# Two sets of expert rows, V's products in two halves, and a new order of small steps, in a fused attention and expert kernel

## The reference

```
h   = layernorm(x)
q   = elu(h Wq) + 1;  k = elu(ctx Wk) + 1;  v = ctx Wv       # 16 heads of 8 features
out_t = (sum over s <= t of (q_t . k_s) v_s) / cumsum(q)_t    # causal, per head, element by element in q
x   = x + out Wo
h2  = layernorm(x)
bids = sigmoid(h2 conf_w' + conf_b) * wealth                  # 8 experts
the two best experts of each token, weights softmax(two best bids)
x   = x + sum over the two of weight * down_e(silu(gate_e h2) * up_e h2)    # inner width 512
```

## Time and profile before

| | us |
|---|---|
| median of 3 runs | 433.47 |
| lowest, highest | 432.7, 433.85 |
| the profiled execution | 430.86 |
| its span, first to last instruction | 429.1 |

### The profile page before, as it was taken

How to read it: one execution, slowest core, us unless ns; L and a number is a source line. 1 busy time by engine, 2 the same in 40 slices (tenths; PEclk the granted TensorE clock), 3 DMA queues, 4 the chain that set the end, 5 groups by cost and what they waited for, 6 DMA issues and landing times.

```text
span 429.1 us, 12428 instructions
## 1 busy us (share of the span) xinstructions
PE 319.4 (74%) x4413; PEld 264.9 (62%) x4413; DVE 288.5 (67%) x769; ACT 217.4 (51%) x440; POOL 212.2 (49%) x342
## 2 busy tenths in 40 slices
PE   3658788785988868586821089999999999999600
PEld 2537475654757756475520079999989989877400
DVE  5476999869796897989518247667657657633345
ACT  2591938347354573933122046766766766644300
POOL 4200223737364375666675406666666667664500
PEclk9896989688755899988555579999999999999855
DMA  8103030411404013010011333233233233221088
GB/s 270 63 2 124 2 124 4 128 48 34 141 15 152 12 33 107 20 33 27 26 44 44 115 49 78 61 74 70 60 76 70 61 72 66 51 51 23 4 273 314
DMA packets 45129, 32.36 MB, mean 75 GB/s; under 512 B 32262, under 2 KB 38796, under 8 KB 45072
## 3 DMA queue, kind: packets, MB, share of 16 engines
q1 hardware_dynamic: 40752, 23.12, 19.6%
q0 software_dynamic: 4320, 8.47, 6.3%
HBM read 15.16 MB, written 12.21 MB: 64 GB/s over the span
## 4 chain that ended last, share of the span: by engine, by line
issue 29%; POOL 28%; DVE 17%; PE 10%; DMA 8%; ACT 3%; SPq 3%; POOLq 1%; DVEq 0%; ACTq 0%
POOL by_token L488 12%; POOL by_expert L421 10%; DMA by_expert<-token_rows,rows_to 4%; DVE Pm L712 3%; DVE Vexp L695 2%; PE scores L954 2%; PE bank L938 2%; DVE stats L647 2%; DMA w_hi<-by_token 2%; POOL y_scale L483 2%; PE bank L970 2%; POOL rstd L392 1%; POOL y_to L484 1%; SPq L347 1%; DVE oT L719 1%
## 5 line engine op out<-in xcount | busy, mean ns | idle before, releaser
L488 POOL DMA_INDIRECT by_token<-y_sb,y_to x71 | 83.3, 1173 | 26.4 <-issue 24.8
L894 DVE TENSOR_TENSOR Kexp<-hid,hid_hi 128x512 f16<-128x512 f32 x71 | 48.8, 688 | 47.9 <-ACT hid_hi L626 47.7
L421 POOL DMA_INDIRECT by_expert<-token_rows,rows_to x64 | 65.1, 1017 | 22.1 <-issue 22.1
L888 DVE SCALAR_TENSOR_TENSOR hid<-scores,silu 128x512 f32<-128x512 f32 x71 | 48.8, 688 | 24.9 <-PE scores L1074 24.9
L619 ACT ACTIVATE silu<-bank 128x512 f32<-128x512 f32 x71 | 42.3, 596 | 34.4 <-PE bank L1074 33.8
L1072 PE MATMUL bank<-xgT,w_hi 128*128 128x256 f16 (+1 forms) x160 | 42.4, 266 | 17.7 <-DMA xgT<-by_expert 16.5
L954 PEld LDWEIGHTS scores<-qT,Kexp 32*128 32x128 f32 x1024 | 39.6, 229 | 25.3 <-DVE Pm L712 22.7
L1089 PE MATMUL bank<-w_hi,hid_hi 128*128 x284 | 51.4, 220 | 2.5 <-DVE Kexp L894 2.5
L954 PE MATMUL scores<-qT,Kexp 32*128 32x128 f32 (+1 forms) x1024 | 44.5, 322 | 10.7 <-DVE Pm L712 10.7
L1091 PE MATMUL bank<-w_hi,Kexp 128*128 x284 | 51.0, 219 | 0.0
L1090 PE MATMUL bank<-w_lo,hid_hi 128*128 x284 | 50.9, 219 | 0.0
(11 more groups left out here) (148 smaller groups left out, 689.2 us busy)
## 6 DMA issues: line engine op xcount, KB each, us to landing
w_raw<-in_w_pack_dram SPq DMA_DIRECT2D x8, 768.0 KB, 4.9
x_all<-in_x_tok_dram SPq DMA_DIRECT2D x8, 256.0 KB, 5.2
cT<-in_ctx_t_dram SPq DMA_DIRECT2D x8, 256.0 KB, 5.4
w_hi<-by_token SPq DMA_DIRECT2D x4, 512.0 KB, 7.2
w_lo<-by_token SPq DMA_DIRECT2D x4, 512.0 KB, 7.6
out_dram<-x_all SPq DMA_DIRECT2D x8, 256.0 KB, 5.8
by_expert<-pad_row SPq DMA_DIRECT2D x9, 130.0 KB, 2.7
by_token<-y_sb,y_to POOLq DMA_INDIRECT x71, 2.7
```

Of the source, the lines that this page charges most:

```text
L421: pool.indirect_dma_start(by_expert, bass.IndirectOffsetOnAxis(ap=rows_to[:, s, b:b + 1], axis=0), token_rows[:, b, s, :], None).then_inc( ...
L488: pool.indirect_dma_start(by_token, bass.IndirectOffsetOnAxis(ap=y_to[:, kk, s:s + 1], axis=0), y_sb[:, kk, s, :], None, bounds_check=NT * ...
L888: dve.scalar_tensor_tensor(hid[:, slot, :], bank[2 + slot], 1.0 / WSCALE, silu[:, slot, :], ALU.mult, ALU.mult).then_inc(hid_done, 1)
L894: dve.tensor_tensor(hid_lo[:, k % 2, slot, :], hid[:, slot, :], hid_hi[:, k % 2, slot, :], ALU.subtract).then_inc(lo_done, 1)
```

## The change

The two buffers `token_rows` and `rows_to` become two each, used by even and odd units in turn, with a semaphore `dispatched` for each. ACT and DVE now wait in the tail of unit u for the dispatch of unit u-2, where they waited for that of unit u-1. ACT's `tail_norm` gets a wait for POOL's `tail_rows` of unit u-2, which reads the `x2hat` that is overwritten. `front_values` is called once for each half: the first half (bank 1) directly behind `values(u, 1)`, the second where the whole was. PE's `tail_x2` goes ahead of `values(u, 1)`. On ACT the first two `front_keys` go ahead of `front_copy_x`, `tail_norm` ahead of the exponentials of q, and `tail_x2` ahead of the last two `front_keys`. DVE's `front_v` waits for each half.

```diff
--- before.py
+++ after.py
@@ -119,12 +119,12 @@
         region = sb("region", [P, E])
         rank = sb("rank", [P, UB, E])
         place = sb("place", [P, TOP, UB, E])
-        rows_to = sb("rows_to", [P, TOP, UB], U32)
+        rows_to = [sb(f"rows_to{i}", [P, TOP, UB], U32) for i in range(2)]
         pair_id = sb("pair_id", [P, UB, TOP])
         unit_ids = sb("unit_ids", [P, UB, TOP])
         unit_start = sb("unit_start", [P, UB, TOP])
-        token_rows = sb("token_rows", [P, UB, TOP, ROW])
-        row_halves = token_rows[:].rearrange("p b s r -> p (b s r)").bitcast(F16).rearrange("p (b s r) -> p b s r", b=UB, s=TOP)
+        token_rows = [sb(f"token_rows{i}", [P, UB, TOP, ROW]) for i in range(2)]
+        row_halves = [rows[:].rearrange("p b s r -> p (b s r)").bitcast(F16).rearrange("p (b s r) -> p b s r", b=UB, s=TOP) for rows in token_rows]
         pad_row = sb("pad_row", [P, ROW])
 
         count = sb("count", [1, E])
@@ -235,7 +235,7 @@
         placing = sem("placing")
         before_done = sem("before_done")
         rows_to_done = sem("rows_to_done")
-        dispatched = sem("dispatched")
+        dispatched = [sem(f"dispatched{i}") for i in range(2)]
         padded = sem("padded")
         count_ps = sem("count_ps")
         pad_at_done = sem("pad_at_done")
@@ -320,7 +320,7 @@
                     sp.wait_ge(x_loaded[par], 16 * ((u - par) // 2) if isinstance(u, int) else 16 * (u // 2))
                 sp.dma_start(x_all[:, bass.ds(u * UB, UB), :], x_tok[:, bass.ds(u * UB, UB), :]).then_inc(x_loaded[par], 16)
                 if not (isinstance(u, int) and u < 2):
-                    sp.wait_ge(v_ps, u - 1)
+                    sp.wait_ge(v_ps, 2 * (u - 1))
                     sp.wait_ge(k_ps, u - 1)
                 sp.dma_start(cT[par][:], ctx_t[:, bass.ds(u * NCH, NCH), :]).then_inc(ctx_loaded[par], 16)
 
@@ -354,7 +354,8 @@
                 if at_least(i, 4):
                     sp.wait_ge(y_to_done, 2 * (i - 3))
                     sp.wait_ge(up_ps, blocks(i - 3))
-                sp.wait_ge(dispatched, 16 * NB * TOP)
+                for rows in dispatched:
+                    sp.wait_ge(rows, 16 * NB * TOP // 2)
                 sp.dma_start_transpose(xgT[:, k, :, 0:size(i) * P], by_expert_halves[bass.ds(at, size(i) * P), 0:2 * D]).then_inc(xgT_loaded[k], 16)
                 sp.dma_start(row_meta[:, k, 0:size(i)], by_expert[bass.ds(at, size(i) * P), D:D + 2].rearrange("(s p) r -> p s r", s=size(i))).then_inc(meta_loaded[k], 16)
 
@@ -403,10 +404,10 @@
 
                 pool.wait_ge(row_hi_done, u + 1)
                 for s in range(TOP):
-                    pool.tensor_tensor(row_halves[:, :, s, D:2 * D], x2hat[par][:], row_halves[:, :, s, 0:D], ALU.subtract).then_inc(row_lo_done, 1)
+                    pool.tensor_tensor(row_halves[par][:, :, s, D:2 * D], x2hat[par][:], row_halves[par][:, :, s, 0:D], ALU.subtract).then_inc(row_lo_done, 1)
                 if not first(u):
                     pool.wait_ge(id_next, u)
-                pool.tensor_tensor(token_rows[:, :, :, D + 1], pair_id[:], unit_start[:], ALU.add).then_inc(row_id_done, 1)
+                pool.tensor_tensor(token_rows[par][:, :, :, D + 1], pair_id[:], unit_start[:], ALU.add).then_inc(row_id_done, 1)
 
             def dispatch(u, batches):
 
@@ -418,8 +419,8 @@
                     pool.tensor_tensor(unit_start[:], unit_start[:], unit_ids[:], ALU.add).then_inc(id_next, 1)
                 for b in batches:
                     for s in range(TOP):
-                        pool.indirect_dma_start(by_expert, bass.IndirectOffsetOnAxis(ap=rows_to[:, s, b:b + 1], axis=0),
-                                                token_rows[:, b, s, :], None).then_inc(dispatched, 16)
+                        pool.indirect_dma_start(by_expert, bass.IndirectOffsetOnAxis(ap=rows_to[u % 2][:, s, b:b + 1], axis=0),
+                                                token_rows[u % 2][:, b, s, :], None).then_inc(dispatched[u % 2], 16)
 
             def body(u, par):
                 if not last(u):
@@ -512,6 +513,8 @@
 
             def tail_norm(u, par):
                 act.wait_ge(shift2_done, u + 1)
+                if u >= 2:
+                    act.wait_ge(row_lo_done, TOP * (u - 1))
                 norm(x2hat[par], u, rstd2, shift2, x2hat_done)
 
             def front_copy_x(u):
@@ -550,9 +553,9 @@
             def tail_rows(u, par):
                 act.wait_ge(x2hat_done, UB * (u + 1))
 
-                if not first(u):
-                    act.wait_ge(dispatched, 16 * UB * TOP * u)
-                act.activation(row_halves[:, :, :, 0:D], x2hat[par][:].unsqueeze(2).to_broadcast([P, UB, TOP, D]), ACT.Copy).then_inc(row_hi_done, 1)
+                if u >= 2:
+                    act.wait_ge(dispatched[par], 16 * UB * TOP * (u // 2))
+                act.activation(row_halves[par][:, :, :, 0:D], x2hat[par][:].unsqueeze(2).to_broadcast([P, UB, TOP, D]), ACT.Copy).then_inc(row_hi_done, 1)
 
             def tail_exp1(u):
                 act.wait_ge(lg_ps, u + 1)
@@ -571,16 +574,18 @@
                     front_norm(u + 1)
                 off_scores(u, 1)
                 if not last(u):
+                    front_keys(u + 1, 1 - par, range(2))
                     front_copy_x(u + 1)
-                    front_keys(u + 1, 1 - par, range(2))
+                if not first(u):
+                    tail_norm(u - 1, 1 - par)
+                if not last(u):
                     front_exp(u + 1, 1)
                 off_scores(u, 2)
                 if not first(u):
-                    tail_norm(u - 1, 1 - par)
+                    tail_x2(u - 1, 1 - par)
                 if not last(u):
                     front_keys(u + 1, 1 - par, range(2, 4))
                 if not first(u):
-                    tail_x2(u - 1, 1 - par)
                     tail_exp1(u - 1)
                 off_scores(u, 3)
                 if not first(u):
@@ -684,8 +689,8 @@
                 dve.scalar_tensor_tensor(qT[par][:], bank[0][:], bq_one[:], expn[:, 1, :], ALU.add, ALU.max).then_inc(qk_done, 1)
 
             def front_v(u, par):
-                dve.wait_ge(v_ps, u + 1)
                 for half in range(2):
+                    dve.wait_ge(v_ps, 2 * u + half + 1)
                     for a in range(2):
                         rows = slice(a * CH, a * CH + CH)
                         cs = slice(half * NCH // 2, (half + 1) * NCH // 2)
@@ -763,10 +768,10 @@
                 dve.wait_ge(vexp_act, u + 1)
                 done(dve.tensor_scalar(vdiff[:], vexp[:], 1.0, None, ALU.add))
                 done(dve.reciprocal(wts[:], vdiff[:]))
-                if not first(u):
-                    dve.wait_ge(dispatched, 16 * UB * TOP * u)
-                dve.tensor_scalar(token_rows[:, :, 0, D], wts[:], 1.0 / WSCALE, None, ALU.mult).then_inc(weights_done, 1)
-                dve.scalar_tensor_tensor(token_rows[:, :, 1, D], wts[:], 1.0 / WSCALE, vexp[:], ALU.mult, ALU.mult).then_inc(weights_done, 1)
+                if u >= 2:
+                    dve.wait_ge(dispatched[u % 2], 16 * UB * TOP * (u // 2))
+                dve.tensor_scalar(token_rows[u % 2][:, :, 0, D], wts[:], 1.0 / WSCALE, None, ALU.mult).then_inc(weights_done, 1)
+                dve.scalar_tensor_tensor(token_rows[u % 2][:, :, 1, D], wts[:], 1.0 / WSCALE, vexp[:], ALU.mult, ALU.mult).then_inc(weights_done, 1)
 
             def tail_place(u):
 
@@ -779,7 +784,7 @@
                 dve.tensor_tensor(before[:], before[:], chosen_sum[:], ALU.add).then_inc(before_done, 1)
                 dve.wait_ge(placing, 3 * u + 3)
                 with nc.allow_low_precision(reason="a row's number is a whole number, exact in any of the types"):
-                    dve.tensor_reduce(rows_to[:], place[:], AX_X, ALU.add).then_inc(rows_to_done, 1)
+                    dve.tensor_reduce(rows_to[u % 2][:], place[:], AX_X, ALU.add).then_inc(rows_to_done, 1)
 
             def weights(u, par, m):
 
@@ -928,12 +933,12 @@
                 pe.wait_ge(xT_copied, u + 1)
                 pe.matmul(bank[0], Wq_s, xT[:], start=True, stop=True).then_inc(q_ps, 1)
 
-            def front_values(u, par):
+            def front_values(u, par, half):
                 pe.wait_ge(ctx_loaded[par], 16 * (u // 2) + 16)
                 if not first(u):
-                    pe.wait_ge(qk_done, 2 * u)
-                for c in range(NCH):
-                    ps = bank[1 - c // 4][:, (c % 4) * P:(c % 4 + 1) * P]
+                    pe.wait_ge(qk_done, 2 * u - 1 + half)
+                for c in range(half * NCH // 2, (half + 1) * NCH // 2):
+                    ps = bank[1 - half][:, (c % 4) * P:(c % 4 + 1) * P]
                     for a in range(2):
                         ins = pe.matmul(ps[a * CH:(a + 1) * CH, :], cT[par][:, c, :], Wv_s, start=True, stop=True)
                 ins.then_inc(v_ps, 1)
@@ -1021,28 +1026,33 @@
                     front_transpose_x(u + 1)
                     front_project_q(u + 1)
```

(22 more changed lines are left out.)

## The result

The changed kernel took 422.01 us in the median of 4 runs (419.31 to 422.75), the kernel before 433.66 us: 0.973 of it, with an interval of 0.9686 to 0.9773. The saving is 11.7 us where 14.9 were forecast, and 418.6 stands against 422.01. The profiled execution took 421.34 us, with a span of 419.6.

The account below looks back on a forecast made before the run. DVE, nearly full in the unit stage, was taken as the bound (PE in body 4); savings 1.7 + 4.2 + 2.5 + 3.5 + 1.0 + 0 + 2.0 = 14.9 us from 433.47 gave 418.6 us, range 413.5 to 426.5.

Parts of the forecast that it names:

- The removed wait: Unit stage, first weight write: waiting for the landing of rows two units back costs nothing; DVE's 10.3 us of waits go.
- The collision: Later bodies: POOL's subtractions L406 stop DVE's weight write L768, 1.1 us a body (bounds 0 and 2.29), making 22.95 us.
- Body 2: Unit stage, body 2: its dispatch starts late, so L406 does not collide; 26.06 to 21.85 us, 4.2 us saved.
- Bodies 6 and 7: Last two bodies: their short waits for landing are replaced by the collision of 1.1 us; 0 saved.
- Body 4: PE-bound body at clock 0.59: 1.7 us saved if the clock stays low, 5.4 if high; middle 3.5 taken.
- Halves: V's products in two halves: 1.7 us saved in body 0; no saving of their own counted in bodies 2, 3, 5.
- ACT's order: ACT's new order: off_scores(u, 2) at most 1.64 us later, about 0.4 us slack left; cost 0, gain 0.
- Tail: After body 7: unit 6's dispatch starts earlier, so the last rstd starts with its statistics; 2.0 us saved.
- Rival A: Bodies 3 to 7: nothing collides and the clock holds; 22.1 us saved, 411.4 us; chance 0.12.
- B: Both subtractions stop DVE in bodies 3 to 7, body 4 stays at the low clock; 7.4 us saved, 426.1 us; chance 0.18.
- C: PE's clock stays low through bodies 1 to 5; 2.9 us slower, 436.4 us; chance 0.03.
- D: DVE's landing wait becomes waiting for PE at tail_o; 5 to 7 us gained, 427 to 428 us; chance 0.03.

Follow-up runs that it names:

- the filler: The changed kernel with extra products of V, results not read, in bodies 6 and 7, against the kernel before: 418.97 us, 0.9737.

## Why the prediction was right, and which steps were off

- **The removed wait: right.** It is gone from the trace, body 3 and body 5 are 23.50 and 23.42 us where 22.95 was said, and no wait for the unit two back appeared.
- **The collision: right in kind, under-sized.** L773 is stretched by 0.65 us in body 1, as in the earlier trace rows. In the others the forecast took 1.1 us. From the first step of `tail_weights` to the row numbers DVE needs 1.37 us when nothing stops it; over that stand 0.65 us in bodies 3, 4 and 6, 1.5 in body 5, 1.85 in body 7 and 2.8 in body 2. That the two really exclude each other is shown by the kernel that holds POOL back. L774, with two inputs in SBUF, stood 2.93 us, through both subtractions and the end of an issue. The rule that the prediction took from the Trainium skill (SBUF — State Buffer, "SBUF: two separate sides") names such steps too, beside a GpSimd operation that reads SBUF. This row agrees with it as to a subtraction, and shows DVE kept out through two in a row. The forecast took one size for two cases. In the kernel before, POOL waited for ACT ahead of all eight pairs; in the changed one it waited ahead of five and came to those of bodies 2, 5 and 7 straight from its last transfer, and these are the three large ones.
- **Body 2: the step that failed.** "L406 comes after DVE's small steps and does not collide", 4.2 us saved. It saved 1.1. POOL had its last transfer done at 80.89, 18.45 us into the body, and DVE asked for L774 at 17.8: the two met in the worst way. I had put POOL's end there from the landing of its rows, and did not work out its issue times. The sum took 0 us for a collision in this body, and the rows show 2.8.
- **Bodies 6 and 7: failed**, 0 forecast, 4.7 us lost. The waits for landing that went were worth 0.8 and 1.2 us there. In their place DVE's first mask of body 7 and the addition of `x` now wait 1.65 and 1.85 us for the chain through PE, whose clock is lower (0.79 and 0.66, where the earlier trace rows has 0.91 and 0.75), and 0.5 us more go in each body to the third mask of body 6 and the second of body 7, which wait for ACT. The stretch of L773 and L769 comes on top. Before, the same bodies took 38.7 us in one trace and 41.0 in the other, so up to half of this loss may be the clock's draw; without the halves they took 41.1, with the filler 40.9.
- **Body 4: the middle (3.5) was near** the 4.1 measured. The clock was 0.86 and not 0.59: the low stretch went, here and in the trace with the filler (1.00), and stood in both of the kernel before. Which part of the change ends it was not settled; without the halves body 4 has 0.93, and body 5 0.79. The 28.33 us also held a collision of 0.96 us (L779 above) that the sum did not count.
- **Halves: right in body 0, missing ahead of it.** Body 0 saved 2.9 us. Without the halves it keeps 1.3 of them (21.71 us against 23.03), so the halves gave 1.6, where 1.7 was forecast. That they clear `tail_o` in full bodies was right too: without them DVE waits there, by the 1.65 and 1.30 us above. But 2.1 us before body 0 were not in the sum at all: the call for unit 1 ahead of the bodies was in the diff, and I had priced only those in the bodies. Body 0 starts at 19.8 to 22.2 us in the eight traces with the halves and at 21.9 to 25.4 in the six without.
- **ACT's order: 0 forecast.** `mask_scores(u, 2)` does wait for `off_scores` in some bodies (0.24, 0.73 and 0.51 us in bodies 2, 4, 6, before only 0.95 in body 4), so the slack was misjudged. It also gave what the sum had left out: the 1.3 us of body 0 that are not the halves'. The order alone shortens body 0 as much (21.78 us, against 23.15 with the buffers alone, both on the first chip). Its 1.4% on that chip, with gaps, is no surer than the other small ratios. What it is worth as a whole without the gaps was not measured.
- **Tail: right.** From `tail_o(7)` to the last `rstd` it is 6.8 us and not 8.75, 2.0 saved as forecast. The steps for it start 0.6 us after POOL is free, with the statistics:

```profile
208.32 0.20 POOL L390 TENSOR_TENSOR nm<-zero,mv 128x4 f32<-128x4 f32 x1 [0.60 <-DVE mv L656]
```

Rival A did not come. B's double stop came in bodies 2, 5 and 7 alone. C and D did not come. The time is inside the forecast's own range (415 to 422.5), by half a microsecond. But it is there in part by luck, because errors cancel. Bodies 2, 6 and 7 fell short by 3.1, 2.0 and 2.7 us, bodies 3 and 5 by 0.5 each and the last stages by 0.55, some 9.4 us in all. The start (2.1), body 0 (1.2) and body 4 (0.6) gave 3.9 us more than forecast: 14.9 - 9.4 + 3.9 = 9.4, the 9.5 us of the spans. The medians differ by 11.7, since the profiled execution of before lay further under its median.

What stays open: how much of the 2.7% each part carries on a chip without gaps. Buffers and order together give 0.4% there by the runs, and the halves on top of them the rest. The traces divide it otherwise: the halves give 3.4 of the 9.5 us, and bodies 2 to 5 took 103.8 and 104.5 us in the two traces of the kernel before, 97.5 without the halves and 96.1 in the changed kernel, so most of what these bodies gained came without the halves. But the trace without the halves is that kernel's fastest run, 4.5 us under its median. The buffers alone were not run there, so their part is read from the traces and not shown by a run. And it is open why the gaps come with the dispatch on two of the chips.

## What to carry to other kernels

A wait that is removed hands its time to the next thing in the same place. Look there for an instruction of another engine that until now came later, and work out the start times of both engines' instructions to half a microsecond, in every body and not in one pattern. A step that is called ahead of the loop as well as in it has two prices. And where a wait hides behind slower hardware, as the landing did in bodies of 31 us, the second buffer is worth nothing: the same edit gave 0 on two chips. And measure the same kernel twice before you believe 1%.

## What the runs showed of the hardware that was not expected

- The same kernel took 433, 459 and 473 us on different chips. In two traces of the changed kernel (spans 419.6 and 461.3 us) 27 of the 42 us between them lie in bodies 2 to 5, which have indirect transfers: 30 to 31 us each where it is 23 to 25. There TensorE has holes of 0.3 to 1.1 us, and VectorE some of 0.9 to 2.4 us, to which the profile gives no releaser. Body 1, without transfers, takes 22.5 us in both. That the transfers cause the holes is not shown.
- VectorE steps of 0.16 us stood 2.93 and 2.02 us, until the second of two GpSimd subtractions in a row had ended, where GpSimd came to the pair within 0.03 us of its last issue (7 of 7 cases); where it had been idle ahead of the pair, they were released after the first (56 of 56). Beside the issue of a transfer alone, steps of the same kind kept their time (0.68 to 0.70 us in 18 cases).
- TensorE's granted clock falls at the same place in the same body of both traces of one kernel (body 4, 0.59), and that low stretch is gone in the four traces without gaps in which the order of its work is another (0.86, 0.93, 1.00 and 1.00).
